# Three attentions of a four-layer trunk: softmax sums and spread reciprocals as 16-bit products of high and low parts, outputs in one buffer

## The reference

```python
# L1x: 64 columns a head, keys and values from the context (77 rows)
# L2a1: 32 columns a head, keys and values from the tokens themselves (128 rows);
#       after the softmax, weights of later keys are set to zero (causal)
# L2a2: 32 columns a head, keys and values from the context (77 rows)
a = softmax(einsum('bshd,bthd->bhst', q, k) * hd ** -0.5, axis=-1)
o = einsum('bhst,bthd->bshd', a, v)
x = x + o.reshape(b, s, 16 * hd) @ Wo + bo
```

## Time and profile before

| | |
|---|---|
| median of 3 runs | 1318.52 us |
| the profiled execution's own time | 1317.21 us |
| its span, first to last instruction | 1315.5 us |
| TensorE busy | 1015.7 us, 77% |
| VectorE busy | 793.2 us, 60% |
| ScalarE busy | 728.0 us, 55% |
| GpSimd busy | 452.8 us, 34% |
| chain that ended last | PE 52%, DVE 22%, ACT 9%, issue 7%, POOL 4%, DMA 3% |
| mean granted clock of TensorE | 0.868 of full |

### The profile page before, as it was taken

The page is one execution under the profiler, slowest core; times in us unless marked ns, Lnnn a source line. Parts: engine busy times, 40 slices in busy tenths (PEclk is TensorE's granted clock), DMA queues, the critical chain, the costliest instruction groups (busy, mean ns, idle before and its releaser), DMA issues.

```text
span 1315.5 us, 38383 instructions
## 1 busy us (share of the span) xinstructions
PE 1015.7 (77%) x15523; PEld 768.1 (58%) x15580; DVE 793.2 (60%) x2107; ACT 728.0 (55%) x1477; POOL 452.8 (34%) x493
## 2 busy tenths in 40 slices
PE   3788577889999955579996679997569976776774
PEld 2455466657778833346774437775457853554663
DVE  4667655765554499577755567656634466766432
ACT  5876354765554453466655556657445575764321
POOL 2566714410111143243232221001460546657132
PEclk9788588999999966689998869999779985987787
DMA  3321122210000010100001000000032212111122
GB/s 99 105 87 43 55 70 70 67 36 18 26 25 28 2 48 17 37 29 11 3 4 41 1 2 3 3 4 1 21 99 80 64 36 70 42 33 31 54 77 75
DMA packets 60299, 53.28 MB, mean 41 GB/s; under 512 B 10655, under 2 KB 48927, under 8 KB 59935
## 3 DMA queue, kind: packets, MB, share of 16 engines
q1 hardware_dynamic: 54353, 41.62, 10.9%
q0 software_dynamic: 4096, 8.40, 2.2%
q10 hardware_dynamic: 1679, 0.81, 0.2%
HBM read 33.90 MB, written 16.25 MB: 38 GB/s over the span
## 4 chain that ended last, share of the span: by engine, by line
PE 52%; DVE 22%; ACT 9%; issue 7%; POOL 4%; DMA 3%; POOLq 1%; ACTq 0%; DVEq 0%; SPq 0%
PE psum L673 18%; PE psum L1184 6%; PE psum L1202 5%; PE psum L842 5%; PE psum L815 3%; PE psum L796 3%; DVE area L1844 3%; POOL sorted_in L2730 2%; PE psum L829 2%; DVE stats L1825 2%; DVE area L1980 2%; PE psum L680 2%; ACT xn L1295 1%; DVE area L2075 1%; PE psum L766 1%
## 5 line engine op out<-in xcount | busy, mean ns | idle before, releaser
L1971 DVE TENSOR_REDUCE negm<-psum 128x4 bf16<-128x308 f32 (+1 forms) x192 | 96.0, 543 | 60.1 <-PE psum L766 59.7
L2459 DVE TENSOR_TENSOR area<-area 128x512 bf16<-128x512 f32 x106 | 73.0, 691 | 96.9 <-ACT area L1742 68.5
L2559 POOL TENSOR_TENSOR moe<-stage,moe 128x512 bf16<-128x512 f32 x47 | 55.1, 1174 | 203.5 <-ACT moe L1266 203.5
L1271 ACT ACTIVATE area<-psum 128x512 bf16<-128x512 f32 (+3 forms) x160 | 77.3, 501 | 83.4 <-PE psum L673 65.9
L1184 PE MATMUL psum<-xT_hi,moe 128*128 128x128 bf16 x848 | 109.7, 228 | 8.3 <-DVE xT_lo L1844 4.5
L1446 ACT ACTIVATE area<-psum 77x1024 f32<-77x1024 f32 (+1 forms) x96 | 92.7, 1017 | 27.7 <-PE psum L796 27.7
L1844 DVE TENSOR_TENSOR area<-psum,area 128x512 bf16<-128x512 f32 (+2 forms) x152 | 83.0, 573 | 40.1 <-ACT area L1271 38.8
L2552 POOL TENSOR_SCALAR rstd<-moments 128x4 f32<-128x4 f32 (+1 forms) x49 | 12.9, 263 | 272.2 <-DVE moments L1829 272.2
L1202 PE MATMUL psum<-moe,area 128*128 x1272 | 105.2, 223 | 1.2 <-DVE area L2468 0.9
L1184 PEld LDWEIGHTS psum<-xT_hi,moe 128*128 x848 | 81.3, 102 | 20.7 <-issue 10.7
L1184 PE MATMUL psum<-xT_lo,moe 128*128 128x128 bf16 x424 | 92.5, 228 | 0.0
(11 more groups left out here) (235 smaller groups left out, 2686.8 us busy)
## 6 DMA issues: line engine op xcount, KB each, us to landing
area<-sorted_in SPq DMA_DIRECT2D x22, 256.0 KB, 3.9
sorted_out<-area SPq DMA_DIRECT2D x22, 256.0 KB, 2.6
stage<-in_w_L0m SPq DMA_DIRECT2D x16, 256.0 KB, 2.8
stage<-in_w_L2m SPq DMA_DIRECT2D x16, 256.0 KB, 2.7
stage<-in_w_L3m SPq DMA_DIRECT2D x16, 256.0 KB, 2.7
sorted_in<-area SPq DMA_DIRECT2D x2, 1472.0 KB, 7.3
stage<-in_w_L2a SPq DMA_DIRECT2D x6, 320.0 KB, 3.9
stage<-in_w_L1x SPq DMA_DIRECT2D x4, 320.0 KB, 3.1
```

The source lines that it names most:

```text
L1271: ins = act.activation(out, bank, ACT.Copy)
L1971: empty(dve.tensor_reduce(K.negm[:, s, 4 * k:4 * k + 4], bank_of(key)[:, 0:4 * L].rearrange("p (h l) -> p h l", h=4), AX.X, ALU.max, negat ...
L2459: dve.tensor_tensor(R.HL[u], R.HF[u], upper(R.HF[u]), ALU.subtract).then_inc(K.tile_split, tiles.one())
```

## The change

The exponentials and the reciprocals get 16-bit high and low parts. The high part is the upper half of each float32 word, read in place (`upper`, every second 16-bit element); the low part is the float32 value less that, rounded to 16 bits: for the exponentials a new GpSimd subtraction of 1024 columns, two a batch; for the reciprocals a new VectorE subtraction of 128 columns behind the reciprocal, which now does not empty the bank itself. Sums and spread become two 16-bit products (high, then low part) where one float32 product was, with `fourths` and the identity in 16 bits. The outputs (L829) stay float32. `ON` and `OT` have one buffer instead of two.

```diff
-        self.fourths = sb("fourths", [128, 4, 32], F32)
+        self.fourths = sb("fourths", [128, 4, 32], BF16)
...
-OT_AT, OT_N = ON_AT + 2 * ON_N, 1024
-RS_AT, RS_N = OT_AT + 2 * OT_N, 128
+OT_AT, OT_N = ON_AT + ON_N, 1024
+RS_AT, RS_N = OT_AT + OT_N, 192
+PL_AT, PL_N = RS_AT + 2 * RS_N, 8 * 64
...
+        self.PH = [upper(v) for v in self.PF]
+        self.PL = [K.carve(PL_AT + PL_N * s, PL_N, BF16) for s in range(4)]
...
-        self.ONs = [K.carve(ON_AT + n_v * s, n_v) for s in range(2)]
-        self.OTs = [K.carve(OT_AT + n_v * s, n_v) for s in range(2)]
-        self.RSs = [K.carve(RS_AT + RS_N * s, RS_N) for s in range(2)]
+        self.ON, self.OT = K.carve(ON_AT, n_v), K.carve(ON_AT + n_v, n_v)
+        self.RF = [K.carve(RS_AT + RS_N * s, 128) for s in range(2)]
+        self.RS = [(upper(v), K.carve(RS_AT + RS_N * s + 128, 64, BF16)) for s, v in enumerate(self.RF)]
...
         def sums(b):
             bank = take(name, "sum", b)
             for r in range(4):
-                for i in range(4):
-                    ins = pe.matmul(bank[32 * i:32 * i + 32, 0:S], K.fourths[0:L, r, :], exponentials_of(b, 4 * r + i, False),
-                                    start=r == 0, stop=r == 3, skip_group_check=True)
+                n, at = 2 * b + r // 2, 4 * S * (r % 2)
+                sem.wait_ge(K.p_split, A.half0 + n + 1)
+                for part in (A.PH, A.PL):
+                    for i in range(4):
+                        ins = pe.matmul(bank[32 * i:32 * i + 32, 0:S], K.fourths[0:L, r, :],
+                                        part[n % 4][0:L, at + S * i:at + S * i + S], start=r == 0 and part is A.PH,
+                                        stop=r == 3 and part is A.PL, skip_group_check=True)
...
         def spread(b):
...
                 for c in range(4):
-                    for i in range(A.heads_in_tile):
-                        r, at = divmod(A.heads_in_tile * (4 * a + c) + i, 4)
-                        row = 32 * at + r
-                        ins = pe.matmul(bank[hd * i:hd * i + hd, S * c:S * c + S],
-                                        K.ident[:, row:row + 1].broadcast_to([128, hd]), A.RSs[b % 2], start=True, stop=True)
+                    for part in range(2):
+                        for i in range(A.heads_in_tile):
+                            r, at = divmod(A.heads_in_tile * (4 * a + c) + i, 4)
+                            row = 32 * at + r
+                            ins = pe.matmul(bank[hd * i:hd * i + hd, S * c:S * c + S],
+                                            K.ident_bf[:, row:row + 1].broadcast_to([128, hd]), A.RS[b % 2][part],
+                                            start=part == 0, stop=part == 1, skip_group_check=True)
...
# scalar_program, outputs(b)
-                if b >= 2:
-                    sem.wait_ge(*K.emptied_at((name, "scale", b - 2, a)))
+                if b >= 1:
+                    sem.wait_ge(*K.emptied_at((name, "scale", b - 1, a)))
...
# vector_program, sums(b)
-            empty(dve.reciprocal(A.RSs[b % 2], bank_of(key)[:, 0:S]), key)
+            chained(dve.reciprocal(A.RF[b % 2], bank_of(key)[:, 0:S]))
+            high, low = A.RS[b % 2]
+            empty(dve.tensor_tensor(low, A.RF[b % 2], high, ALU.subtract), key)
# vector_program, outputs(b)
-                if b >= 2:
-                    sem.wait_ge(K.filled, K.fill[name, "out", b - 2])
+                if b >= 1:
+                    sem.wait_ge(K.filled, K.fill[name, "out", b - 1])
...
# gpsimd_program
+        def exponentials_lo(b, half):
+            n = 2 * b + half
+            sem.wait_ge(K.exp_done, A.half0 + n + 1)
+            pool.tensor_tensor(A.PL[n % 4][0:A.L], A.PF[n % 4][0:A.L], A.PH[n % 4][0:A.L], ALU.subtract).then_inc(K.p_split, 1)
...
-            if 0 <= b - 2 < B and A.keys_from_x:
-                mask(b - 2, 0)
+            if 0 <= b - 2 < B:
+                exponentials_lo(b - 2, 0)
+                if A.keys_from_x:
+                    mask(b - 2, 0)
             if ahead + 1 < NG and b % GB == 3:
                 rstd(slice(0, 128), group(ahead + 1))
-            if 0 <= b - 2 < B and A.keys_from_x:
-                mask(b - 2, 1)
+            if 0 <= b - 2 < B:
+                exponentials_lo(b - 2, 1)
+                if A.keys_from_x:
+                    mask(b - 2, 1)
```

19 lines of the change are left out of this document (9 added, 10 removed).

## The result

The changed kernel took **1347.7 us** (median of 4 runs, 1343.9 to 1351.0) against 1318.9 for the kernel before on the same chip: the ratio is **1.021** (95% interval 1.018 to 1.025), 29 us slower. The forecast was 1310, and its range ended at 1323. The profiled execution took 1343.9 us with a span of 1342.1, 26.6 more than the 1315.5 of before. The page's busy times (us, share of the span, instructions) show the exchange: TensorE 1015.7 to 994.6 us, VectorE 793.2 to 845.3, GpSimd 452.8 to 634.4.

The account below looks back on a forecast made before the run. TensorE was taken to bound the three attentions, its time counting almost fully, with GpSimd nearly free. L1x -14.6, L2a1 +0.8 and L2a2 +5.0 sum to -8.8 us: 1308.4 on the profile's scale, 1310 on the runs', range 1284 to 1323.

Parts of the forecast that it names:

- TensorE's products: Sums and spread in the three attentions: 16-bit products save TensorE 1.45 us a batch in L1x, 0.84 at 32 columns.
- rival 3: Sums and spread: weight loads, not columns, set TensorE's pace, so TensorE gains nothing; +38 us, 1356; chance 8%.
- GpSimd's subtraction, 1.90 us: Exponentials' low part on GpSimd, two a batch: each 1024-column subtraction takes 1.90 us, ends 1.09 and 2.2.
- The subtraction on VectorE waits for the instruction in flight: Behind the reciprocal: the 0.28 us subtraction waits for GpSimd's one running instruction, then gets in, ending 0.13 us after it.
- Rivals 1 and 2: VectorE's subtraction: gets in early in L2a2 and L2a1, 1288, 22%; or no port wait for this form, 1278, 12%.
- Plain batches: Ordinary batches of each attention: L1x 10.2 to 9.0 us, L2a1 6.8 to 7.1, L2a2 6.5 to 7.6.
- Buffers, fourths: nothing: Single ON and OT buffers add only waits already satisfied by program order, and 16-bit fourths cost nothing: no change.
- L2a2, +5.0 us: Stage L2a2: the subtraction's wait outweighs the spread's saving, +1.18 us in six batches; stage total +5.0 us.
- L1x, -14.6 us: Stage L1x, 64 columns a head: TensorE savings less a 0.28 us wait, 1.17 us a batch without projections; total -14.6 us.
- L2a1, +0.8 us: Stage L2a1, with masks on GpSimd: subtraction wait, queue at start and drain, against savings in other iterations; total +0.8 us.

Follow-up runs that it names:

- one_psum: Changed kernel with one operand of the new VectorE subtraction read from the sums' PSUM bank instead of SBUF (spread low half numerically wrong); ratio 0.988 to the kernel before.
- halved: Changed kernel with each GpSimd subtraction of 1024 columns made as two of 512; ratio 0.994 to the kernel before.
- filled_idle: Changed kernel with 26 extra 16-bit TensorE products ahead of the second half's row maxima, in 13 iterations of L2a2 alone; ratio 1.013 to the kernel before.
- before_pause: Kernel before, with VectorE taking each L2a2 batch's reciprocal three times before releasing the bank of the sums; ratio 1.041 to the kernel before.
- pause_filled: The before_pause kernel with 26 extra 16-bit TensorE products ahead of the second half's row maxima in L2a2; ratio 1.039 to the kernel before.
- pool_alone: Kernel before, plus GpSimd's two subtractions a batch (awaited by the sums, results unused) and single output and scale buffers; ratio 1.006 to the kernel before.

## Why the prediction was wrong

- *TensorE's products*: right. Sums to the next group 0.47 us for 0.45 forecast (the timeline of L1x above); rival 3, the loads setting the pace, did not happen. Eight groups in 0.47 us are 0.059 us a group. The rule of the Trainium skill ("TensorE: Matmul & The Clock Gate", section "LDWEIGHTS (loading the stationary operand)"), taken for four loads one after another, would have made it 0.107, by estimate, and the measurement decides.
- *GpSimd's subtraction, 1.90 us*: 1.89.
- *The subtraction on VectorE waits for the instruction in flight*: right in each stage's plain batches, 1.08, 1.15 and 2.04 us for 1.05, 1.1 and 2.0, and shown from both sides by one_psum and halved. Rivals 1 and 2 fell with that; L2a2 did not flip. The Trainium skill ("SBUF — State Buffer", section "Who interferes with whom") says that a tensor_tensor with both inputs in SBUF contends with GpSimd's reads; these runs agree (2.04 us with both in SBUF, 0.29 with one in PSUM).
- *Plain batches*: L1x 9.17 (9.0 forecast), L2a1 7.10 (7.1). L2a2's 7.6 is right for the full clock: 7.54 in filled_idle, with the same wait. In the changed kernel the one plain batch at full clock had a shorter wait (7.20), and the others took 8.0 to 9.6.
- *Buffers, fourths: nothing*: right for the buffers. The fourths' type was not tried apart.
- *L2a2, +5.0 us*: **this is the step that failed**; it was +20.2. The sum priced 0.24 to 2 us of idle TensorE time at its own length. Behind such idle time the granted clock fell to 1.2 GHz, and the products after it took longer: 9.18 us for a batch whose wait costs 7.54 at full clock. Of the 25.6 us between the changed kernel and one_psum 16.1 at most are the wait, so some 9.5 or more are this. The earlier trace rows showed a clock of 0.96 to 1.00 in the stages and the text took it as given. before_pause and pause_filled are the proof that the idle time does it: the kernel before loses its clock, too, when VectorE holds the bank, and keeps it in the plain batches when the time is filled. A smaller part failed otherwise: in iterations 5, 6 and 9 the subtraction was to get in early and save 0.84 us each. It took 1.66, 1.23 and 1.56 us, and these batches, at full clock, were 0.3, 0.7 and 0.2 us longer than before; that is 3.6 of the 15.2 us missed.
- *L1x, -14.6 us*: it was -6.0, by the same step. The plain batches were near (1.0 us saved for 1.17). But the three iterations in which the outputs stand behind the reciprocal, forecast at 0.6 us less each, took 13.73, 14.73 and 13.13 us, 1.0, 2.6 and 1.3 more than before, at clocks of 0.88, 0.77 and 0.87. That is 6.8 us of the 8.6 missed. In one of them TensorE waited 1.48 us at 337 us (0.71 before), and the outputs behind it took 3.09 us instead of 1.97:

```profile
336.57 0.29 DVE L1992 TENSOR_TENSOR area<-area 128x128 bf16<-128x128 f32 x1
336.91 3.09 PE L837 MATMUL psum<-area 77*64 77x128 f32 x32 [1.48 <-DVE area L1992]
```

  How much of this is lost differs between executions. In filled_idle, whose L1x has the same code, TensorE waited 1.48 us in the same place and kept the clock. The busy time of this batch, in the changed kernel and in filled_idle:

```profile
334.10:348.83 14.73, 13.25 (x210) 10.40 (x209) 7.49 (x22) 6.61 (x12) 6.17 (x6) 0.77 0.06 20
342.78:354.61 11.83, 10.35 (x211) 8.07 (x210) 7.12 (x22) 6.37 (x12) 6.17 (x6) 1.00 0.09 25
```

  The subtraction took 0.29 us here and did not wait for GpSimd at all. The reciprocal begins 1.51 us after the sums in both kernels, because VectorE is busy until then; the sums are 0.45 us shorter and the subtraction adds 0.32, which is the 0.77 us that TensorE idles longer. Time saved ahead of a wait on another engine was turned into idle time.
- *L2a1, +0.8 us*: it was +6.2. The plain batches were right; the start and the drain of GpSimd's queue, put at +1.0 and +1.7, measured 5.7 alone (pool_alone), part of it again at a clock of 0.85. The mechanism was named and its size was wrong. Another 2.4 us are the second batch, with 1.96 us of idle TensorE time and a clock of 0.82: the step that failed in L2a2.
- *Left over*: 6.2 us of the span in stages with unchanged code. Such stages varied by as much between profiles of unchanged code (L3x from 143.4 to 148.9 us), so they show nothing for or against the change.

## What to carry to other kernels

Where TensorE is nearly always busy, a wait put in its way costs its length and then the clock: price both, from a stretch of the trace at each level, and ask of each edit that makes TensorE's work shorter which wait it uncovers. The small VectorE instruction with both inputs in SBUF waited here for the whole GpSimd instruction in flight, 1.89 us long; what helped was to read one input from PSUM, to cut the GpSimd instruction in two, or to release what the others wait for before it. And take a change apart by stage: GpSimd's low parts cost one of three attentions 5.7 us and the others nothing that the profiles tell, and the stages' lengths measured apart added up when they were put together. Take more than one profile, too, before a difference of 3 us in a stage is explained.

## What the hardware showed that I had not expected

- After idle time of some 1.5 to 2.3 us a batch the granted clock of TensorE alternated between its levels in L2a2 (0.81 in one batch, 1.00 in the next), with the same instructions in both. All four batches with 2.29 us of idle time had a clock of 0.81 or 0.82, the one with 1.85 us had 1.00, and so had the four of L2a1 with 1.37 to 1.41. In between it isn't settled: after 1.48 us in one place of L1x the clock was 0.77 in two profiles (changed, one_psum) and 1.00 in a third (filled_idle).
- Filling idle time with products kept the clock (7.54 us instead of 9.18 for a plain batch, 8.36 instead of 9.91), though more was computed. As the filling itself costs time where the stop comes before it, neither stage got shorter by more than 1.7 us.
- A VectorE subtraction of 128 columns takes 0.29 us with one input in PSUM as with both in SBUF; only the wait tells them apart.
